# Residuals of q and k, scaled y and the fp8 bias moved from VectorE to ScalarE and GpSimd

## The reference, cut to what matters

```
zn  = layernorm(z) * ln_scale + ln_bias
q, k, v = zn @ w_qkv                        # 16 heads of 8 features
att = softmax(q k^T / sqrt(8)) v            # per head, 512 x 512 scores
out = z + att @ w_proj + b_proj             # first layer
y   = bf16(layernorm(...))                  # input of the second layer
y_q = fp8_e4m3(y / s_in);  k_q = fp8_e4m3(kernel / s_k)
f   = bf16((y_q @ k_q) * (s_in * s_k)) + bias    # second layer
```

## Time and profile before

| What | Value |
|---|---|
| median of three runs | 1521.89 us |
| profiled execution | 1519.24 us, span of its trace 1517.5 us |
| PE busy | 1223.0 us (81%) |
| DVE busy | 1236.9 us (82%) |
| ACT busy | 963.4 us (63%) |
| POOL busy | 845.3 us (56%) |
| mean granted TensorE clock | 0.92 |
| attention turns in steady state | 54.7 to 58.0 us each, about 130 to 860 us of the span |

### The profile page before, as it was taken

One profiled execution on the slowest core, in us unless ns is written; L12 is line 12 of the kernel. 1 busy time (PEld: TensorE's weight loads), 2 busy tenths in 40 slices (PEclk: granted clock), 3 DMA queues, 4 the chain that ended last, 5 costly groups with the idle time before them and its releaser, 6 DMA issues.

```text
span 1517.5 us, 25374 instructions
## 1 busy us (share of the span) xinstructions
PE 1223.0 (81%) x8528; PEld 490.8 (32%) x8528; DVE 1236.9 (82%) x2629; ACT 963.4 (63%) x1621; POOL 845.3 (56%) x1051
## 2 busy tenths in 40 slices
PE   1398999998998998998998999547878877878862
PEld 0022222322222232232232232213544444544542
DVE  2588789999899999889999995453899898898863
ACT  1067767777766777776776788345775675675630
POOL 5224355555555655555655643534677776776663
PEclk9999889999999999999999999677999999999975
DMA  1243033023123123113113200000000000000000
GB/s 38 29 89 50 13 39 49 16 37 50 22 31 50 26 26 51 31 21 50 35 18 51 31 14 2 1 0 0 1 8 15 8 8 14 8 8 15 8 8 21
DMA packets 46992, 37.58 MB, mean 25 GB/s; under 512 B 8080, under 2 KB 44816, under 8 KB 46864
## 3 DMA queue, kind: packets, MB, share of 16 engines
q1 hardware_dynamic: 42256, 29.65, 11.6%
q0 software_dynamic: 4608, 6.32, 2.7%
HBM read 6.04 MB, written 4.19 MB: 7 GB/s over the span
## 4 chain that ended last, share of the span: by engine, by line
PE 29%; DVE 25%; POOL 16%; issue 13%; DMA 7%; SPq 6%; ACT 4%; POOLq 0%; ACTq 0%; DVEq 0%
DVE neg_max L484 10%; PE bank L197 8%; PE bank L178 7%; DMA k_stack<-k_parts 6%; SPq L617 6%; PE bank_pair L165 4%; PE bank L206 3%; PE bank L267 2%; POOL probs L1130 2%; DVE probs L892 2%; ACT probs L341 2%; PE bank L714 2%; POOL rs_x L1064 1%; PE bank_pair L706 1%; POOL x_all L1124 1%
## 5 line engine op out<-in xcount | busy, mean ns | idle before, releaser
L484 DVE TENSOR_REDUCE neg_max<-bank_pair 128x2 f32<-128x1024 f32 x512 | 610.6, 1214 | 86.5 <-PE bank_pair L165 82.9
L341 ACT ACTIVATE probs<-bank 128x512 f32<-128x512 f32 x1024 | 559.4, 595 | 150.3 <-PE bank L178 146.3
L178 PE MATMUL bank<-q_stack,k_stack 50*128 50x512 bf16 x1024 | 369.1, 405 | 10.3 <-ACT probs L341 4.0
L165 PE MATMUL bank_pair<-k_stack,q_stack 48*128 48x512 bf16 x1024 | 309.8, 414 | 70.1 <-DMA k_stack<-k_parts 39.8
L197 PE MATMUL bank<-probs,v_pad 128*32 128x256 f32 x4096 | 344.2, 411 | 0.7 <-ACT outT L305 0.4
L178 PEld LDWEIGHTS bank<-q_stack,k_stack 50*128 50x128 bf16 x1024 | 83.6, 94 | 277.2 <-ACT probs L341 220.6
L706 PE MATMUL bank_pair<-probs,w_gates 128*128 128x512 f32 x256 | 133.4, 670 | 20.2 <-DVE probs L1022 17.3
L197 PEld LDWEIGHTS bank<-probs,v_pad 128*32 128x32 f32 x4096 | 83.4, 110 | 183.4 <-issue 181.3
L1022 DVE SCALAR_TENSOR_TENSOR probs<-v_pad,conv_w,probs 128x512 f32<-128x512 f32 x96 | 98.0, 1059 | 6.3 <-ACT probs L856 5.6
L706 PE MATMUL bank_pair<-probs,w_in 128*128 128x512 f32 x128 | 67.2, 651 | 31.3 <-ACT probs L856 28.5
L165 PEld LDWEIGHTS bank_pair<-k_stack,q_stack 48*128 48x128 bf16 x1024 | 54.2, 95 | 101.2 <-DVE neg_max L484 57.4
(11 more groups left out here) (224 smaller groups left out, 2219.4 us busy)
## 6 DMA issues: line engine op xcount, KB each, us to landing
q_stack<-q_parts SPq DMA_DIRECT2D x192, 64.0 KB
k_stack<-k_parts POOLq DMA_DIRECT2D x96, 64.0 KB, 4.5
k_stack<-k_parts SPq DMA_DIRECT2D x96, 64.0 KB
x_all<-in_z_dram SPq DMA_DIRECT2D x16, 256.0 KB, 2.8
out_dram<-x_all SPq DMA_DIRECT2D x16, 256.0 KB, 2.3
q_stack<-max_rows SPq DMA_DIRECT2D x64, 8.0 KB
w_gates<-in_w_gates_dram SPq DMA_DIRECT2D x1, 512.0 KB, 3.8
w_in<-in_w_in_dram SPq DMA_DIRECT2D x1, 256.0 KB, 2.9
```

Source lines behind the costliest of these rows:

```text
L165: mm = nc.tensor.matmul(score_ps[c % 2][:, h, :], q_stack[bpar][rows, j, c * P:(c + 1) * P], k_stack[bpar][rows, j, :], start=True, stop=True)
L178: nc.tensor.matmul(st_ps[h][:, :], k_stack[par][rows, p, c * P:(c + 1) * P], q_stack[par][rows, p, :], start=True, stop=True).then_inc(s[" ...
L341: nc.scalar.activation(probs[:, (p // 2 % 2) * 4 * C + (2 * (p % 2) + h) * C + c, :], st_ps[h][:, :], ACT.Exp, scale=SCALE).then_inc(s["ex ...
L484: nc.vector.tensor_reduce(neg_max[j // 4][:, c, j % 4, :], score_ps[c % 2][:, :, :], AX_X, ALU.max, negate=True).then_inc(s["max_read"], 1)
```

## The change

ACT copies q (and k) a second time from the bank, in fp32, into `q_rest` (`k_rest`), right behind its rounding to part 0. POOL then subtracts part 0 from this copy, in place. DVE does nothing for q and k. The bank `misc` is freed by ACT's second copy.

POOL scales y right after making it, ahead of its split of k. POOL adds the fp8 bias, between the norm of batch i+2 and `z_res`. Its casts to part 1 have two operands (times 1.0, times 1.0) in place of one. In the norm of the attention output, the two broadcast operations over 512 columns become four two-operand operations over 128 columns each, after a small one that negates the mean. PE's instructions keep their order.

```diff
 ACT, slots 11 and 14
                 nc.scalar.activation(parts[:, 0, :], misc[:, :], ACT.Copy).then_inc(s[n + "_hi"], 1)
+                wait(act, s[n + "_lo"], 3 * (i + 2))
+                nc.scalar.activation(rest[:, :], misc[:, :], ACT.Copy).then_inc(s[n + "_hi"], 1)
 DVE
-            if slot == 4 and live(i, -2):
-                b = i - 2
-                wait(dve, s["ffn_read"], b + 1)
-                wait(dve, s["x2_step"], 10 * b)
-                nc.vector.tensor_tensor(f_b[:, :, :], f_bf[:, :, :],
-                                        consts["ffn_bias"][:, :].unsqueeze(1).to_broadcast([P, C, D]), ALU.add)\
-                    .then_inc(s["ffn_biased"], 1)
...
-            if slot in (12, 15) and live(i, 2):
-                n, parts, rest = ("q", q_parts, q_rest) if slot == 12 else ("k", k_parts, k_rest)
-                wait(dve, s[n + "_hi"], i + 2 + 1)
-                wait(dve, s[n + "_lo"], 2 * (i + 2))
-                nc.vector.tensor_tensor(rest[:, :], misc[:, :], parts[:, 0, :], ALU.subtract)\
-                    .then_inc(s[n + "_r"], 1)
             q = s["quant_step"]
             if slot == 0 and live(i, -2):
                 b = i - 2
-                wait(dve, s["y_step"], 4 * (b + 1))
-                nc.vector.tensor_scalar(y_scaled[:, :], y_bf[:, :, :].rearrange("p c d -> p (c d)"),
-                                        consts["s_in_inv"][:, 0:1], None, ALU.mult).then_inc(q, 1)
-                wait(dve, q, 10 * b + 1)
+                wait(dve, s["scaled_ready"], b + 1)
 POOL
+        if live(i, -2):
+            b = i - 2
+            wait_apart(gp, s["ffn_read"], b + 1, past_wait)
+            wait_apart(gp, s["x2_step"], 10 * b, past_wait)
+            TT(f_b[:, :, :], f_bf[:, :, :], consts["ffn_bias"][:, :].unsqueeze(1).to_broadcast([P, C, D]), ALU.add)\
+                .then_inc(s["ffn_biased"], 1)
...
-            wait_apart(gp, s[n + "_r"], b + 1, past_wait)
-            TS(parts[:, 1, :], rest[:, :], 1.0, None, ALU.mult).then_inc(s[n + "_lo"], 1)
-            wait_apart(gp, s[n + "_lo"], 2 * b + 1, past_wait)
+            wait_apart(gp, s[n + "_hi"], 2 * (b + 1), past_wait)
+            TT(rest[:, :], rest[:, :], parts[:, 0, :], ALU.subtract).then_inc(s[n + "_lo"], 1)
+            wait_apart(gp, s[n + "_lo"], 3 * b + 1, past_wait)
+            TS(parts[:, 1, :], rest[:, :], 1.0, 1.0, ALU.mult, ALU.mult).then_inc(s[n + "_lo"], 1)
+            wait_apart(gp, s[n + "_lo"], 3 * b + 2, past_wait)
             TT(parts[:, 2, :], rest[:, :], parts[:, 1, :], ALU.subtract).then_inc(s[n + "_lo"], 1)
...
-            TT(att_c[:, :, :], att[:, :, :], per_token(mv_b[:, :, 0]), ALU.subtract).then_inc(q, 1)
-            TT(att_c[:, :, :], att_c[:, :, :], per_token(t(1)), ALU.mult).then_inc(q, 1)
+            TT(t(2), mv_b[:, :, 0], neg_one, ALU.mult).then_inc(q, 1)
+            for c in range(C):
+                TS(att_c[:, c, :], att[:, c, :], tiny[:, 2, c:c + 1], tiny[:, 1, c:c + 1], ALU.add, ALU.mult)\
+                    .then_inc(q, 1)
...
+            wait_apart(gp, q, at0 + 4, past_wait)
+            wait_apart(gp, s["quant_step"], 9 * b, past_wait)
+            TS(y_scaled[:, :], y_bf[:, :, :].rearrange("p c d -> p (c d)"), consts["s_in_inv"][:, 0:1], 1.0,
+               ALU.mult, ALU.mult).then_inc(s["scaled_ready"], 1)
```

More of the change, by code:

```diff
@@ L137, in attention_phase @@
              "stat_b_raw stat_b x1_step stat_c_raw stat_c y_step quant_step yT_ps yT_ready ffn_ps ffn_read "
-             "ffn_biased stat_d_raw stat_d x2_step").split()
+             "scaled_ready ffn_biased stat_d_raw stat_d x2_step").split()
     s = {n: sem(n) for n in names}
@@ L146, in attention_phase @@
             ("o1", -1, s["o_nat_ready"], 2, 2), ("maxT1", 0, s["maxT_read"], 2, 2), ("oT", -1, s["oT_ready"], 1, 1),
[L147 to L148 removed]
+            ("proj", -1, s["att_ready"], 1, 1), ("znT", 2, s["znT_ready"], 1, 1), ("q", 2, s["q_hi"], 2, 2),
+            ("o0", 0, s["o_nat_ready"], 2, 1), ("maxT0", 1, s["maxT_read"], 2, 1), ("k", 2, s["k_hi"], 2, 2)]
     def wait_misc_free(pe, i, name):
@@ L222, in side_product @@
             if slot == 2 and live(i, -2):
-                wait(pe, s["quant_step"], 10 * (i - 2) + 5)
+                wait(pe, s["quant_step"], 9 * (i - 2) + 4)
                 wait_misc_free(pe, i, "yT")
@@ L324, in side_read @@
             if slot in (11, 14) and live(i, 2):
-                n, parts = ("q", q_parts) if slot == 11 else ("k", k_parts)
+                n, parts, rest = ("q", q_parts, q_rest) if slot == 11 else ("k", k_parts, k_rest)
                 wait(act, s[n + "_ps"], i + 2 + 1)
@@ L392, in side @@
                 wait(dve, s["zres_step"], 3 * (b + 1))
-                wait(dve, s["x1_step"], 5 * b)
+                wait(dve, s["x1_step"], 8 * b)
                 nc.vector.tensor_tensor(att[:, :, :].rearrange("p c d -> p (c d)"), misc[:, :],
@@ L405, in side @@
                 b = i - 2
-                wait(dve, q, 10 * b + 2)
+                wait(dve, q, 9 * b + 1)
                 nc.vector.tensor_scalar(y_grid[:, :], y_grid[:, :], 2.0 ** -6, 1.5 * 2.0 ** 20, ALU.max, ALU.mult)\
@@ L410, in side @@
                 b = i - 2
-                wait(dve, q, 10 * b + 3)
+                wait(dve, q, 9 * b + 2)
                 nc.vector.tensor_tensor(y_sum[:, :], y_scaled[:, :], y_grid[:, :], ALU.add).then_inc(q, 1)
@@ L414, in side @@
                 b = i - 2
-                wait(dve, q, 10 * b + 4)
+                wait(dve, q, 9 * b + 3)
                 wait(dve, s["yT_ps"], b)
@@ L453, in between @@
                 b = i - 2
-                wait(dve, q, 10 * b + 6)
+                wait(dve, q, 9 * b + 5)
                 nc.vector.tensor_scalar(y_absmax[:, :], y_absmax[:, :], 464.0, 464.0, ALU.max, ALU.subtract)\
@@ L458, in between @@
                 b = i - 2
-                wait(dve, q, 10 * b + 7)
+                wait(dve, q, 9 * b + 6)
                 nc.vector.tensor_scalar(y_absmax[:, :], y_absmax[:, :], 1e30, 1e30, ALU.mult, ALU.mult)\
@@ L463, in between @@
                 b = i - 2
-                wait(dve, q, 10 * b + 9)
+                wait(dve, q, 9 * b + 8)
                 wait(dve, s["x2_step"], 10 * b)
@@ L468, in between @@
                 b = i - 1
-                wait(dve, s["x1_step"], 5 * (b + 1))
+                wait(dve, s["x1_step"], 8 * (b + 1))
                 wait(dve, s["y_step"], 4 * b)
@@ L494, in pool @@
             b = i + 1
-            wait_apart(gp, s["k_lo"], 2 * (b + 1), past_wait)
+            wait_apart(gp, s["k_lo"], 3 * (b + 1), past_wait)
             wait_apart(gp, s["st_ready"], 64 * b - 64, past_wait)
@@ L582, in pool @@
             wait_apart(gp, q, at0 + 3, past_wait)
-            TT(att_c[:, :, :], att_c[:, :, :], per_token(t(1)), ALU.mult).then_inc(q, 1)
-            wait_apart(gp, q, at0 + 4, past_wait)
+            wait_apart(gp, s["zn_ready"], min(b + 4, NB) if isinstance(b, int) else b + 4, past_wait)
+            for c in range(C):
+                TS(att_c[:, c, :], att[:, c, :], tiny[:, 2, c:c + 1], tiny[:, 1, c:c + 1], ALU.add, ALU.mult)\
+                    .then_inc(q, 1)
+            wait_apart(gp, q, at0 + 7, past_wait)
             TT(x_of(b), x_of(b), att_c[:, :, :], ALU.add).then_inc(q, 1)
@@ L613, in sync @@
                                                       (s["k_lo"], k_parts, k_stack[1 - par], K_PART, 1)):
-                wait_apart(sp, done, 2 * (b + 1), past_wait)
+                wait_apart(sp, done, 3 * (b + 1), past_wait)
                 for h in range(halves):
```

9 lines of the change are left out of this document (3 added, 6 removed).

## The result

The changed kernel took 1537.04 us, median of nine runs (1532.62 to 1542.73), beside 1522.07 us for the kernel before on the same chip (1509.69 to 1527.61). The ratio is 1.0093, with a 95% interval of 1.0069 to 1.0117: slower by 0.9%, where no change had been forecast, and 1 us above the range. The profiled span grew from 1517.5 to 1537.4 us, by 19.9 us.

The account below looks back on a forecast made before the run. Stack transfers and DVE's chain were taken to bound slots 0 to 6 nearly equally; -12.5 - 1.4 + 11.9 - 1.3 = -3.3 us gave a median of about 1519 us, no measurable change, range 1496 to 1536 us.

Parts of the forecast that it names:

- What bounds the kernel: Slots 0 to 6: stack transfers (20 to 23 us) and DVE's chain limit at nearly the same height.
- POOL's transfers: Slot 15: they start 0.2 to 2.5 us later against SP's but stay the earlier ones, costed at nothing.
- three signs: Prediction wrong if transfers land earlier with unchanged order, ACT's copies find idle time, or the clock falls at another place.
- ACT's copies: Ahead of the exponentials of slots 12 and 15: 0.85 us per batch (0.4 to 1.1), +11.9 us in fourteen turns.
- DVE's relief: Slots 0 to 6: 3.27 us per batch leave DVE, worth 0.96 us (0 to 2.2); -12.5 us over thirteen turns.
- POOL's prices: On POOL: subtraction 1.15 us, two-operand cast about 0.6, scaling 0.6 to 1.5, bias 1.0; bias and norm cost nothing.
- The tail: Tail turns: scaling leaves DVE, POOL's bias is longer, four-piece norm saves; about -1.3 us, from -3 to +3.
- The range: Whole kernel: 1496 to 1536 us, about 0.8 inside; with the ends of the terms 1500 to 1533 us.
- four terms: Slots 0 to 6 -12.5 us, turn 15 -1.4, ACT +11.9, tail -1.3; sum -3.3 us.
- Rival 1: DVE is the bound after all: 2.9 us per batch come off fourteen turns, 1493 us; chance 0.2.
- Rival 2: Gaps in slots 12 to 15 make PE's clock fall, products taking about double: 1540 to 1561 us; chance 0.14.
- Rival 3: Slot 0: POOL blocks DVE through the shared port, y_grid over 1.1 us in most batches; 1531 us; chance 0.14.

Follow-up runs that it names:

- e1: Kernel before with one added two-operand cast of 0.6 us on POOL ahead of k's split, so its k transfers start later; ratio 1.0091.
- e5: Changed kernel with the scaling of y back on DVE, all else as changed; ratio 0.9977 to the kernel before.
- e10: Changed kernel with SP's transfers reordered: lower half of q, then k, then upper half of q; ratio 0.9905 to the kernel before.
- e7: Kernel before with ACT's fp32 copies of q and k added into an unused tile, subtraction still on DVE; ratio 1.0049.
- e4: Changed kernel with the subtractions for q and k back on DVE, without ACT's fp32 copies; 1491.87 us, ratio 0.9829 to the kernel before.
- e8: Kernel before with the bias on POOL, two-operand casts and four-piece norm; scaling and subtractions stay on DVE; ratio 0.9856.
- e2: Kernel before with only POOL's casts of q and k made two-operand; ratio 0.9914.

## Why the prediction was wrong, step by step

**What bounds the kernel: right.** The reading that transfers and DVE's chain end slots 0 to 6 at nearly the same height, and that relief of DVE turns into a wait for the stacks, is what the waits show. The forecast was 30 us in twelve batches; it became 47.0. DVE's `o_nat` ended at 554.31 + 0.43 = 554.74, 21.2 us after SP's first transfer and 1.7 us before the stacks. DVE's timeline there:

```profile
553.92 0.35 DVE L360 RECIPROCAL rowsum_inv<-bank 128x32 f32<-128x32 f32 x1
554.31 0.43 DVE L364 TENSOR_TENSOR o_nat<-bank,rowsum_inv 128x256 f32<-128x256 f32 x1
```

**POOL's transfers: this step failed.** It said that they "start 0.2 to 2.5 us later against SP's" and that, since they stay ahead of SP's own k transfers, "I cost them at nothing". The start held at +0.53 us, and POOL's transfers did stay the earlier ones (17.5 us beside 23.1 for SP's). The price of nothing did not hold: with POOL's start later, SP's own set ended later, at 23.12 us in place of 21.81 over all twelve turns. The part to the transposes went from 24.34 to 24.93 us, +0.59, where the forecast had it at -0.96: an error of 1.55 us per turn. Over the twelve turns that is 18.6 us of the 23.2 us between the forecast's -3.3 and the profile's +19.9 (by the medians the miss is 1537.04 - 1519 = 18 us). Three runs carry it. With the start alone later (e1) the part grows by 0.89 us; with the scaling taken from ahead of it in the changed kernel (e5) it shrinks by 1.25; with no other edit than SP's order (e10) by 2.09. The claim that the transfers "need 20 to 23 us whatever DVE does" looked at DVE alone; how long they need hangs on when POOL starts its share. None of the three signs that the prediction named for its being wrong allowed for this: they look for an earlier landing, idle time behind the copies or a fall of the clock elsewhere.

**ACT's copies: right in place and nearly in size.** Forecast +0.85 us per turn, between 0.4 and 1.1; the rest of the turn grew by 1.07 us in the change and 0.98 in e7. In turns in which the clock does not fall in it, it is 30.14 us in the kernel before and 30.94 in e7 and e5, which have the copies: +0.80. The change has no such turn; its other 0.27 us go with the clock, which stood at 1.2 GHz for 4.7 us of the rest in place of 4.0. ACT's rows in slots 11 and 12, beside the earlier trace rows:

```profile
520.35 0.60 ACT L329 ACTIVATE q_parts<-bank 128x512 bf16<-128x512 f32 x1 [0.43 <-PE bank L267]
520.84 0.59 ACT L331 ACTIVATE q_rest<-bank 128x512 f32<-128x512 f32 x1
521.32 2.17 ACT L343 ACTIVATE probs<-bank 128x512 f32<-128x512 f32 x4
```

The copy moves the exponentials by 521.32 - 520.84 = 0.48 us, and PE has the wait that follows from it, in slot 12 and again in slot 15. Slot 14 gives a little back, 0.82 us for the 1.01 of the earlier trace rows. PE's timeline:

```profile
521.98 0.39 PE L178 MATMUL bank<-q_stack,k_stack 50*128 50x512 bf16 x1 [0.56 <-ACT probs L343]
...
528.39 0.39 PE L206 MATMUL bank<-ident_bf,max_parts 128*16 128x128 bf16 x4 [0.82 <-DVE max_parts L379]
...
532.62 0.39 PE L178 MATMUL bank<-q_stack,k_stack 50*128 50x512 bf16 x1 [0.56 <-ACT probs L343]
```

**DVE's relief: its worth is not shown by itself.** Where POOL's start is early and ACT has no copies, the part to the transposes falls by 1.18 us (e4, e8: 23.16), a little over the 0.96 forecast. But 0.86 us of that come with the casts alone (e2), where DVE keeps all its operations, so the near agreement is in part luck. A second gain wasn't in the sum: in e4 and e8 the clock stands at 1.2 GHz for 3.1 and 2.8 us a turn, in the kernel before for 6.5, in the change for 7.1. Without a fall the rest is 30.14 us in all three of before, e4 and e8, so the 0.63 and 0.82 us by which it is shorter on average come with the clock. How much of the gain ahead of the transposes does, I can't separate.

**POOL's prices: right.** Two-operand cast 0.62 us (forecast 0.6), subtraction 1.16 (1.15), scaling 0.69 (from 0.6 to 1.5), bias 1.15 (1.0). That the early places cost nothing was right for the bias and the norm, as e8 shows. The groups of POOL's instructions, 200 to 900 us (busy us, mean ns), have them:

```profile
L522 POOL TENSOR_TENSOR f_b<-f_bf,ffn_bias 128x512 bf16<-128x512 bf16 x13 | 15.0, 1152 | 6.3 <-ACT f_bf L350 6.3
...
L560 POOL TENSOR_TENSOR k_rest<-k_rest,k_parts 128x512 f32<-128x512 f32 x12 | 14.0, 1164 | 0.0
...
L598 POOL TENSOR_SCALAR y_scaled<-y_bf,s_in_inv 128x512 f32<-128x512 bf16 x12 | 8.3, 692 | 1.3
...
L562 POOL TENSOR_SCALAR k_parts<-k_rest 128x512 bf16<-128x512 f32 x12 | 7.4, 619 | 1.1
```

**The tail** was put at -1.3 us; since twelve turns account for the whole difference, it and turns 0, 1 and 15 came to about nothing together. I didn't take them apart.

**The range.** The ends of the four terms, added, reach from 1494 to 1538 us, not from 1500 to 1533. The measured 1537.04 lies just inside the former, by the room that the other terms leave; the part ahead of the transposes came out past its own end, +0.59 us where the worst case was 0.

**The rivals.** Rival 1 (DVE is the bound, 1493 us) came out wrong for this change, yet its time is that of e4 (1492 us), which relieves DVE of bias and scaling without the two moves for the rests. That is a coincidence of numbers: the rival's 2.9 us per turn less ACT's 0.85 is not how e4 gets there: its gain has the earlier start of POOL and less time at 1.2 GHz in it. Rival 2 gave the right side by the wrong mechanism. In the twelve turns of the change each fall of the clock lies between 21 and 34 us behind SP's first transfer, so in none of them in slots 12 to 15, which come behind 44 us. Its price was high as well: behind a fall a product took 0.63 us in place of 0.39, which is not double, and a fall of 6.8 us in the rest made it 2.6 us longer (32.7 for 30.14 in the kernel before). Rival 3 asked for `y_grid` above 1.1 us in most batches; its mean was 0.47 us in the change, by the groups of DVE's instructions:

```profile
L435 DVE TENSOR_SCALAR y_grid<-y_scaled 128x512 uint32<-128x512 uint32 x12 | 5.6, 470 | 0.0
```

**What stays open:** why the landing depends on POOL's start as it does. Kernels with a mean offset of 2.6 to 3.3 us land at 21.9 to 22.4 us, those at 4.0 to 6.7 at 23.0 to 23.9 and the kernel before, at 3.5, between them, unless SP serves the lower halves first. Over all twelve turns it is 21.4 to 22.1 us for the first, 21.8 for the kernel before, which is no longer between, and 22.6 to 23.5 for the last. Within one kernel the landing differs by 3 us and more from turn to turn, so these means are rough. A collision of the two sets of transfers in the same DMA engines, in whatever order those take them, would be of this kind; no run here separates that from other ways.

## What to carry to other kernels

When two queues fill the same buffer, a set that ends early can still make the other one end later: give the start of each a price of its own, and before putting work ahead of a transfer on its issuing engine, try the delay alone. Relief of an engine that shares the bound with a transfer is worth only the distance to that transfer, so move the work to where it doesn't stand ahead of it, as e4 and e8 do. Take a many-part edit apart: here the casts alone gain 0.9%, bias and norm perhaps a little more (the intervals of e2 and e8 overlap), and the two moves for the rests cost it all.
